# Largest eigenvalue by eleven matrix squarings in place of sixteen, with moved set-up loads and exchanged PSUM banks, in a two-layer graph kernel

## The reference, cut to what matters

```python
h = relu(layernorm(x));  x = x + layer0(h, adj, ...)      # x is (16, 512, 128), adj is (512, 512)
h = relu(layernorm(x));  x = x + layer1(h, adj, adj, ...)

def layer0(x, adj_mx, alpha_train, w, d, fc_in_w, fc_in_b):
    x0 = x
    h = einsum('bnd,ed->bne', x, fc_in_w) + fc_in_b
    alph = sigmoid(alpha_train)[:, None]
    w_eff = w * clip(d, 0, 1) @ w.T
    for _ in range(8):
        h = h + dt * (alph * 0.5 * (adj_mx @ h - h) + h @ w_eff - h + x0)
    return h

def layer1(x, L, adjacency, ...):
    lam_max = eigvalsh(L)[-1] + 1e-08                      # the largest eigenvalue of a 512x512 matrix
    L_norm = 2.0 * L / lam_max - eye(N)
    h = relu(layernorm((L_norm @ x) @ Wc + bc, g1, be1)); x1 = h + x
    q, k, v = (split_heads(x1 @ W) for W in (Wq, Wk, Wv))  # 4 heads of 32
    attn = softmax(where(adjacency > 0, q @ k.T / sqrt(32), -1e9))
    x2 = layernorm(x1 + (attn @ v) @ Wo + bo, g2, be2)
    return layernorm(x2 + gelu(x2 @ W1 + b1) @ W2 + b2, g3, be3)
```

## Time and profile before

| | |
|---|---|
| median of 3 runs | 951.16 us (950.97 to 957.17) |
| the profiled execution | 951.66 us, of which the span of the trace is 949.9 us |
| PE busy | 884.3 us (93%) |
| DVE busy | 650.7 us (69%) |
| ACT busy | 551.3 us (58%) |
| POOL busy | 325.0 us (34%) |
| mean granted PE clock | 0.984 of full speed |

### The profile page before, as it was taken

How to read it: one execution, slowest core, us unless ns; L and a number is a source line. 1 busy time by engine, 2 the same in 40 slices (tenths; PEclk the granted TensorE clock), 3 DMA queues, 4 the chain that set the end, 5 groups by cost and what they waited for, 6 DMA issues and landing times.

```text
span 949.9 us, 19236 instructions
## 1 busy us (share of the span) xinstructions
PE 884.3 (93%) x6854; PEld 723.6 (76%) x6854; DVE 650.7 (69%) x2075; ACT 551.3 (58%) x1210; POOL 325.0 (34%) x426
## 2 busy tenths in 40 slices
PE   5999999999999999987999999999999999888993
PEld 4878989898989888985677776767777777667782
DVE  5955453535354554635888888888989888886786
ACT  3223343434343332314888888888888887885574
POOL 3211111111111132301445445555555543313876
PEclk9999999999999989999999999999999999999998
DMA  3000000000000000230545555444445555500222
GB/s 97 1 12 12 12 12 13 11 12 12 12 12 12 12 23 1 70 65 18 128 124 133 135 134 135 118 110 110 107 106 122 134 134 134 135 2 2 56 57 67
DMA packets 47232, 61.73 MB, mean 65 GB/s; under 512 B 4377, under 2 KB 22050, under 8 KB 47138
## 3 DMA queue, kind: packets, MB, share of 16 engines
q1 hardware_dynamic: 46034, 60.38, 24.9%
q10 hardware_dynamic: 1104, 0.13, 0.1%
HBM read 39.53 MB, written 20.97 MB: 64 GB/s over the span
## 4 chain that ended last, share of the span: by engine, by line
PE 17%; DVE 11%; POOL 9%; issue 9%; ACT 7%; DVEq 0%; POOLq 0%; ACTq 0%
PE bank L1730 5%; DVE prob L1901 4%; PE bank L1750 3%; PE bank L1794 2%; ACT prob L1841 2%; POOL z_gain L317 2%; POOL z_norm L321 2%; POOL x_bo L1674 2%; PE bank L1717 2%; POOL rstd_b L202 1%; DVE z_std L298 1%; PE bank L353 1%; POOL rstd L202 1%; PE bank L349 1%; ACT probT L1830 1%
## 5 line engine op out<-in xcount | busy, mean ns | idle before, releaser
L1841 ACT ACTIVATE prob<-prob,low 128x512 f32<-128x512 f32 x256 | 184.0, 719 | 58.7 <-DVE low L1901 56.8
L1901 DVE CUSTOM_DVE_ANT_0 prob<-bank,mask 128x512 f32<-128x512 f32 x256 | 171.4, 684 | 27.6 <-PE bank L1717 26.2
L1730 PE MATMUL bank<-ident,prob 128*128 128x128 f32 x1024 | 162.1, 281 | 13.2 <-ACT probT L1830 12.9
L1730 PEld LDWEIGHTS bank<-ident,prob 128*128 128x128 f32 x1024 | 114.2, 141 | 59.0 <-issue 30.8
L1717 PE MATMUL bank<-k_stack,q_stack 128*128 128x512 f32 x256 | 122.6, 480 | 2.3 <-DVE low L1901 1.1
L809 PE MATMUL bank<-B_hi,halves 128*128 128x384 f32 x384 | 106.7, 339 | 0.7 <-DVE halves L1164 0.7
L1830 ACT ACTIVATE probT<-bank 128x512 f32<-128x512 f32 x176 | 102.4, 582 | 3.1 <-PE bank L1730 1.6
L780 PE MATMUL bank<-halves,P3T_hi 128*128 128x256 f32 x512 | 98.1, 293 | 3.4 <-DVE halves L1182 2.2
L963 ACT ACTIVATE Sq<-bank,trace_inv 128x512 fp32r<-128x512 f32 x64 | 43.9, 686 | 87.4 <-PE bank L764 87.4
L601 POOL TENSOR_SCALAR var_eps<-mv 128x4 f32<-128x4 f32 x16 | 3.6, 226 | 261.9 <-DVE mv L1115 261.9
L780 PEld LDWEIGHTS bank<-halves,P3T_hi 128*128 128x128 f32 x512 | 83.7, 198 | 6.3 <-DVE halves L1182 2.5
(11 more groups left out here) (251 smaller groups left out, 1964.3 us busy)
## 6 DMA issues: line engine op xcount, KB each, us to landing
k_stack<-bounce_q SPq DMA_DIRECT2D x64, 256.0 KB, 5.1
q_stack<-bounce_k SPq DMA_DIRECT2D x64, 256.0 KB, 7.5
bounce_q<-k_parts SPq DMA_DIRECT2D x16, 512.0 KB, 2.7
bounce_k<-q_parts SPq DMA_DIRECT2D x16, 512.0 KB, 3.3
x_in<-in_x_dram SPq DMA_DIRECT2D x16, 256.0 KB, 2.8
out_dram<-probT SPq DMA_DIRECT2D x16, 256.0 KB, 2.3
y<-in_adj_dram SPq DMA_DIRECT2D x4, 256.0 KB, 4.5
W1s<-in_L_gnn_W_dram SPq DMA_DIRECT2D x1, 128.0 KB, 2.6
```

Source lines behind the costliest of these rows:

```text
L1730: last = pe.transpose(psum[2 + u % 2][:, mt * P:(mt + 1) * P], prob[u % RING][:, mt * P:(mt + 1) * P], ident[:, :])
L1841: act.activation(prob[u % RING][:, :], prob[u % RING][:, :], ACT.Exp, bias=low[:, u % TURNED:u % TURNED + 1], scale=-1.0, accum_out=row_su ...
L1901: dve.tensor_tensor_reduce(prob[u % RING][:, :], psum[u % 2][:, :], mask[:, u // HEADS, :], 1.0, 3e38, ALU.add, ALU.min, low[:, u % TURNED ...
```

## The change

1. **Eleven squarings.** Six of them (q = 1 to 6) square S - c*I instead of S, where c is 0.45 times an estimate of the largest eigenvalue (the sum of the squared row sums over the sum of the row sums). ACT's copy of a row now also accumulates its row sums into `v` (`power_rows`). The trace of a shifted squaring brings three numbers over PE, and DVE makes seven more instructions on them, four of them on the diagonal blocks of the matrix; PE's first row of the squaring waits for all. Pairs 0 to 4 have 8 rows each and pair 5 has 4. The row sums at `LAM_PAIR` fall away.
2. **Set-up.** `alpha`, `d` and `fc_b` are loaded as six rows of 512 bytes and transposed by PE, one instruction more on PE and one copy on DVE. The spreading of the nine rows (PE and DVE) goes ahead of P3, into banks 4 to 6.
3. **Layer 1.** Spread uses bank 5 and q bank 4; the waits follow. The fourth tile of `normalise` goes from u = 15 to u = 0 of the next round; `split_b2` goes from round 16, u = 13 to round 15, u = 11.

```diff
 PAIRS = BATCH // 2
-ROWS_FIRST = ("T1a", "T2a", "C0a", "C1a", "T1b", "T2b", "C0b", "C2b")
-ROWS_3 = ("T1a", "Y1_0", "Y1_1", "T2a", "Y0_1", "C0a", "C1a", "C2a", "T1b", "T2b", "C0b", "C2b")
-ROWS_2 = ("T1a", "Y1_1", "T2a", "Y0_0", "C1a", "T1b", "T2b", "C1b")
-SQUARES = (ROWS_FIRST, ROWS_3, ROWS_3, ROWS_3, ROWS_3, ROWS_2)
-TRACES = (("T0a", "C3a"), *[("T0a", "Y0_0", "C3a")] * 4, ("T0a", "C0a"))
+ROW_PLACES = ("T1a", "T2a", "C0a", "C1a", "T1b", "T2b", "C0b", "C2b")
+SQUARES = (ROW_PLACES,) * 5 + (ROW_PLACES[:NT],)
+TRACES = (("T0a", "C3a"),) * 5 + (("T0a",),)
 LAST_SQUARED = len(SQUARES) - 1
 SQUARINGS = sum(len(rows) for rows in SQUARES) // NT
 LAM_PAIR, KEY_PAIR = LAST_SQUARED + 1, LAST_SQUARED + 2
-assert SQUARINGS == 2 * PAIRS and KEY_PAIR == PAIRS - 1
+SHIFT = 0.45
+SHIFTED = range(1, SQUARINGS - 4)
+assert KEY_PAIR == PAIRS - 1 and 2.0 ** (SQUARINGS - len(SHIFTED)) * (2 / (1 - SHIFT)) ** len(SHIFTED) >= 2.0 ** 16
...
                 pe.wait_ge(ident_ready, 1)
+                pe.wait_ge(small_loaded, 16 * 3)
+                pe.transpose(psum[6][:, 0:NT + 2], small_rows[:, :], ident[0:NT + 2, 0:NT + 2]).then_inc(setup_psum, 1)
                 pe.wait_ge(w_loaded, 16)
                 pe.transpose(psum[4][:, 0:D], w_in[:, :], ident[:, :]).then_inc(setup_psum, 1)
...
+                pe.wait_ge(B_step, STEPS + 1)
+                pe.wait_ge(one.rows_loaded, 16 * ROWS)
+                row_flat = one.row_in[:, :, :].rearrange("o r d -> o (r d)")
+                for c in range(3):
+                    if c == 2:
+                        pe.wait_ge(U_ready, GROUP)
+                    cols = min(N, ROWS * D - c * N)
+                    pe.matmul(psum[4 + c][:, 0:cols], ones[0:1, :], row_flat[:, c * N:c * N + cols], start=True,
+                              stop=True).then_inc(one.rows_spread, 1)
                 pe.wait_ge(PT_lo_ready, 2 * NT)
                 for mt in range(NT):
                     node_power(mt, P2T_parts, P3_psum)
...
+                pe.wait_ge(one.rows_copied, 3)
...
+                        cols = 3 if q in SHIFTED else 1
                         pe.wait_ge(trace_part_ready, q + 1)
-                        pe.matmul(SQ_BANK[:, 0:1], ones[:, :], trace_part[:, :], start=True,
+                        pe.matmul(SQ_BANK[:, 0:cols], ones[:, :], trace_part[:, 0:cols], start=True,
...
                     if step == (0, "T1a"):
-                        pe.wait_ge(v_ready, 1)
+                        pe.wait_ge(square_ready, NT * SQUARINGS)
...
                 act.dma_start(w_in[:, :], w).then_inc(w_loaded, 16)
-                act.dma_start(d_in[:, :], d.rearrange("(p o) -> p o", o=1)).then_inc(small_loaded, 16)
-                act.dma_start(alpha_in[:, :], alpha.rearrange("(t p) -> p t", p=P),
-                              allow_slow_non_contiguous=True).then_inc(small_loaded, 16)
-                act.dma_start(b_in[:, :], fc_b.rearrange("(p o) -> p o", o=1)).then_inc(small_loaded, 16)
+                act.dma_start(small_rows[0:NT, :], alpha.rearrange("(t p) -> t p", p=P)).then_inc(small_loaded, 16)
+                act.dma_start(small_rows[NT:NT + 1, :], d.rearrange("(o p) -> o p", o=1)).then_inc(small_loaded, 16)
...
                         if mt == 0:
-                            act.wait_ge(trace_step, 3 * q + 3)
-                        act.activation(Sq[1 - s][:, mt, :], SQ_BANK[:, :], ACT.Copy,
-                                       scale=trace_inv2[:, 0:1]).then_inc(square_ready, 1)
+                            act.wait_ge(trace_step, scales_until(q + 1))
+                        act.activation(Sq[1 - s][:, mt, :], SQ_BANK[:, :], ACT.Identity, scale=trace_inv2[:, 0:1],
+                                       accum_out=v[:, mt:mt + 1]).then_inc(square_ready, 1)
...
-                dve.wait_ge(small_loaded, 16 * 3)
-                dve.tensor_scalar(d_clip[:, :], d_in[:, :], 0.0, 1.0, ALU.max, ALU.min).then_inc(dve_setup, 1)
+                dve.wait_ge(setup_psum, turned_small)
+                dve.tensor_copy(small[:, :], psum[6][:, 0:NT + 2]).then_inc(dve_setup, 1)
                 dve.wait_ge(dve_setup, 1)
+                dve.tensor_scalar(d_clip[:, :], d_in, 0.0, 1.0, ALU.max, ALU.min).then_inc(dve_setup, 1)
...
+                dve.wait_ge(setup_psum, product_w)
+                dve.tensor_copy(W, psum[5][:, 0:D]).then_inc(power_ready, 1)
                 dve.wait_ge(alpha_exp, 1)
...
-                                         ALU.mult, ALU.add, trace_part[:, :]).then_inc(trace_part_ready, 1)
+                                         ALU.mult, ALU.add, trace_part[:, 0:1]).then_inc(trace_part_ready, 1)
+                dve.wait_ge(setup_psum, second_U)
+                dve.tensor_copy(U[:, :, 2], psum[6][:, 0:NT]).then_inc(U_ready, 1)
+                for c in range(3):
+                    cols = min(N, ROWS * D - c * N)
+                    dve.wait_ge(one.rows_spread, c + 1)
+                    dve.tensor_copy(one.bc_all[:, :, :].rearrange("p r d -> p (r d)")[:, c * N:c * N + cols],
+                                    psum[4 + c][:, 0:cols]).then_inc(one.rows_copied, 1)
                 for i in range(STEPS):
                     for j in range(STEPS - i):
...
-                    if q is not None:
-                        dve.wait_ge(trace_psum, q + 1)
-                        dve.tensor_scalar(trace[:, :], SQ_BANK[:, 0:1], TINY, None, ALU.max).then_inc(trace_step, 1)
-                        dve.wait_ge(trace_step, 3 * q + 1)
+                    if q is None:
+                        return
+                    done = scales_until(q)
+                    dve.wait_ge(trace_psum, q + 1)
+                    dve.tensor_scalar(trace[:, :], SQ_BANK[:, 0:1], TINY, None, ALU.max).then_inc(trace_step, 1)
+                    dve.wait_ge(trace_step, done + 1)
+                    at_least(dve, square_ready, NT * q)
+                    if q in SHIFTED:
+                        dve.scalar_tensor_tensor(out=mean_power[:, :], in0=trace[:, :], scalar=1.0 / N,
+                                                 in1=SQ_BANK[:, 1:2], op0=ALU.mult, op1=ALU.max
+                                                 ).then_inc(trace_step, 1)
                         dve.reciprocal(trace_inv[:, :], trace[:, :]).then_inc(trace_step, 1)
-                        dve.wait_ge(trace_step, 3 * q + 2)
-                        at_least(dve, square_ready, NT * q)
+                        dve.wait_ge(trace_step, done + 2)
+                        dve.reciprocal(mean_inv[:, :], mean_power[:, :]).then_inc(trace_step, 1)
+                        dve.wait_ge(trace_step, done + 3)
+                        dve.tensor_tensor(out=trace_inv2[:, :], in0=trace_inv[:, :], in1=trace_inv[:, :],
+                                          op=ALU.mult).then_inc(trace_step, 1)
+                        dve.wait_ge(trace_step, done + 4)
+                        dve.tensor_scalar(neg_shift[:, :], SQ_BANK[:, 2:3], mean_inv[:, 0:1], -SHIFT, ALU.mult,
+                                          ALU.mult).then_inc(trace_step, 1)
+                        dve.wait_ge(trace_step, done + 6)
+                        for t in range(NT):
+                            own = Sq[q % 2][:, t, t * P:(t + 1) * P]
+                            dve.scalar_tensor_tensor(out=own, in0=ident[:, :], scalar=neg_shift[:, 0:1],
+                                                     in1=own.bitcast(F32), op0=ALU.mult, op1=ALU.add
+                                                     ).then_inc(trace_step, 1)
+                    else:
+                        dve.reciprocal(trace_inv[:, :], trace[:, :]).then_inc(trace_step, 1)
+                        dve.wait_ge(trace_step, done + 2)
                         dve.tensor_tensor(out=trace_inv2[:, :], in0=trace_inv[:, :], in1=trace_inv[:, :],
                                           op=ALU.mult).then_inc(trace_step, 1)
...
                         dve.wait_ge(square_ready, NT * (q + 1))
+                        if q + 1 in SHIFTED:
+                            dve.tensor_reduce(trace_part[:, 1:2], v[:, :], AX.X, ALU.add)
+                            dve.tensor_tensor_reduce(scratch4[:, :], v[:, :], v[:, :], 1.0, 0.0, ALU.mult, ALU.add,
+                                                     trace_part[:, 2:3])
                         dve.tensor_tensor_reduce(diagonal[:, :, :], diagonal_of(Sq[1 - s]).bitcast(F32), ident_tiles,
-                                                 1.0, 0.0, ALU.mult, ALU.add, trace_part[:, :]
+                                                 1.0, 0.0, ALU.mult, ALU.add, trace_part[:, 0:1]
...
-AT_Y_MOMENTS, AT_H = 9, (11, 12, 13, 15)
+AT_Y_MOMENTS, AT_H = 9, (11, 12, 13)
...
-AT_W1_LO, AT_SPLIT_B2 = (BATCH, 5), (BATCH, 13)
+AT_W1_LO, AT_SPLIT_B2 = (BATCH, 5), (BATCH - 1, 11)
...
                             pe.wait_ge(rinv_ready, e + 1)
-                            pe.wait_ge(x1T_ready, min(r + 1, BATCH) if isinstance(r, int) else r + 1)
```

(13 more changed lines are left out.)

69 lines of the change are left out of this document (28 added, 41 removed).

## The result

The changed kernel takes 922.61 us (median of 4 runs, 921.45 to 925.83) against 953.27 for the kernel before on the same chip, a ratio of 0.968 (95% interval 0.966 to 0.971), about 30 us less. The profiled execution is the longest of the four, 925.83 us with a span of 924.0; the other three have spans of 919.6 to 921.0.

The account below looks back on a forecast made before the run. PE was taken to bound the kernel, busy without a break in layer 0. The terms summed to -33.0 us, giving 918.7 against the profiled 951.66, or 918.2 by the runs' median, stated as 918; range 910 to 930.

Parts of the forecast that it names:

- Five squarings fewer: Layer 0, PE: each squaring with its trace is worth 4.19 us, so five give -21.0 us.
- rival (2): Squarings covered more than they cost: PE meets waits the rows hid, half of 21 us returns; about 931 us, chance 0.09.
- DVE's chain at shifted squarings: Layer 0: PE waits for DVE's chain of about 2.2 us, mostly covered by `first_power`; +0.6 us; `C2_lo` ready near 330.5, needed near 330.8.
- Row sums at pair 6: Pair 6: DVE's 2.28 us reduction goes, so PE's product with S starts earlier; -1.8 us.
- The clock at pair 6: Pair 6: without the 1.8 us idle, the low-clock stretch has half its length; -1.6 us, bounds 0 and -3.3.
- Spreading moved: Set-up: PE's 1.41 us wait for `P3T_lo` ahead of the spreading goes; -1.4 us, bounds 0 and -3.1.
- Small loads: Set-up: row loads land earlier, so PE's first adjacency transposes start near 8.2 instead of 10.06; -1.8 us.
- Layer 1: Layer 1 rounds: most of the spread's wait for `x1T`, 6.4 us over 14 rounds, is gained; -4.5 us.
- rival (1): Small terms are given back: layer 1 waits for `probT` instead, the clock stays low as long; 927 us, chance 0.17.
- split_b2: Round 16: PE's 1.71 us idleness behind this DVE work goes; -1.5 us, bounds 0 and -3.3.
- Rival (3): Layer 0: stops ahead of shifted rows bring the 0.50 clock level for pairs 0 to 3; over 951 us, chance 0.02.
- my last sentence: Prediction is wrong if PE waits over 0.5 us at shifted squarings, `q_lo` waits appear, or low-clock windows between 60 and 300 us.

Follow-up runs that it names:

- No shift: The changed kernel with the six shifts left out, so eleven plain squarings; median 922.08 us.
- Spread dealt: The changed kernel with one spreading product behind each of P3's first three tiles, DVE's copies likewise; ratio 0.972 to the kernel before.
- three: The changed kernel with pair 5's rows in its b half, the quotient's instructions ahead of DVE's first Y1 sum, spreading dealt through P3; median 920.38 us.
- S dealt: The changed kernel with pair 6's S products dealt out between `first_power`'s products and the quotient's instructions ahead of DVE's first Y1 sum; median 929.20 us.
- U mixed: The changed kernel with the one-column products with U and the spreading products dealt out between P3's products; median 924.03 us.

## Why the prediction was right, and which steps were off

The time came 4.6 us above the forecast of 918 and inside the range; against before, about 30 us less where 33 were forecast. Of the 7.1 us that the profiled execution falls short (25.9 against 33.0), 1.7 lie in set-up and pair 0, 1.8 in pair 5 and 3.7 in pair 6.

- **Five squarings fewer: right, 19.1 instead of 20.4 us.** Pairs 1 to 4 gave 4.16 us each. The step that was off is "one squaring with its trace is worth 4.19 us" for pair 5: there it gave 2.44, for the four rows left in the a half uncovered two waits in the b half. This is rival (2) in small, in the one pair with an empty half; with the rows moved it gives 3.80.
- **DVE's chain at shifted squarings: right mechanism, cost 0 instead of 0.6.** I worked it out as 2.2 us; it took 1.9, and left 0.65 us. The `C2_lo` margin held. No shift confirms it by 0.03 us over four pairs.
- **Row sums at pair 6: right, about 1.4 instead of 1.8 us.** The product with S starts 0.22 us behind the last `first_power` matmul. With half of the low stretches taken off, pair 6 took 51.8 us before (55.20 with 6.8 at 0.50) and takes 50.4 now (55.54 with 10.2). The time was not all kept: the quotient behind it is set by DVE's order and POOL's statistics, which I had not followed. "Ask what is late next" was left out at this step.
- **The clock at pair 6: half a hit.** In five of the runs the low stretch is 3.4 us, as I took it, and pair 6 takes 52.0 to 52.2 us, 3.1 less than before (forecast 3.4). In the profiled execution it is 6.8 + 3.4 us, pair 6 is as long as before, and that alone is 3.4 of this profile's shortfall. The bounds were wide enough, the assumption that one execution stands for all was not.
- **Spreading moved: the wait right, the clock wrong.** "What goes is PE's wait of 1.41 us" came true, and at equal clock the move is worth 1.5 us (seven kernels against three). But the product itself doubled its time, 4.20 for 2.20, and P3 behind it ran its first 5 us at half speed. I had named the lengthened weak stretch and then priced it at nothing; the 3.4 us more at 0.50 cost 1.7. From P2 to pair 1 it took 68.9 us against 68.6, so nothing is left of the 1.4 in this profile. Four of the other kernels in this order had 6.8 us more than before. Spread dealt has 68.2 (89.17 - 21.02), by its clock and not by its order.
- **Small loads: the number right, by two misses that cancel.** P2 starts at 20.89 instead of 22.70 us, 1.81 less, as forecast; 19.7 to 21.3 in the other runs with the new loads, 23.70 in the one with the old, which has 3.4 us at 0.50 ahead of P2. But the transposes of the adjacency matrix start at 7.10, not near 8.2, and below the 7.7 that I took for a floor: its loads landed 3.4 us after their issue by the median, where they took 4.5 before. Of these 2.96 us, 1.15 are lost again by P2 (13.79 us from there instead of 12.64, both with 2.0 us idle); the sum had no term for that, and its cause stays open. The row loads were all there at 5.05 us, not at the 6.0 to 6.5 that I took. From the fixed cost of about 2.0 us in the Trainium skill, "DMA: Bandwidth & Descriptors", section "Anatomy of one DMA — SWDGE (gpsimd) path", I had estimated 4.1. The -2.4 of that estimate is not what this profile shows, but P2's start scatters by 1.6 us over the twelve kernels with the new loads, more than the difference.
- **Layer 1: right, 3.75 instead of 4.2 us for 13 rounds.** 0.29 us a round instead of 0.32. The `probT` wait did not take it back, which answers rival (1), and no wait for `q_lo` appeared.
- **split_b2: right, about 2.0 instead of 1.5 us** in round 16. The other 1.0 of the 3.0 us by which round 16 fell goes with the low stretch of the earlier trace rows, which round 16 no longer has; round 15 gives back 1.1 us, and whether this edit has a part in that is open.
- **Rival (3), a low level over the squarings: not seen.** The trace has 1.00 from 60 to 300 us although PE's rows wait in one bank. The short idle times that the Trainium skill describes ("TensorE: Matmul & The Clock Gate", section "A second HAM failure mode: psum-queue depth-cycling") hardly occurred here, 0.35 us in 240, so its rule was not put to the test. In nine of the other twelve kernels a stretch of 3.4 us starts between 63.2 and 66.2 us, in pair 0, as one did in the kernel before at 55.2; by the letter of my last sentence this would have counted against the forecast, and it costs 1.5 us (pair 0 37.6 instead of 36.1).

## What to carry to other kernels

A piece of work taken off the busiest engine is worth its own time only where the rest of that stretch never waits; look at the place it leaves, half pair by half pair, and put what remains where the waits are. Follow a released wait to the next consumer's whole chain, on other engines too (here DVE's order and POOL's statistics), before it is counted. When an engine's clock changes within a run, first take half of its low stretches off the stages where it is never idle, and only then compare: here this turned ranges that lay over each other (68.6 to 72.0 and 68.7 to 70.4) into two groups, each at most 0.3 us wide, and 1.5 us apart. Totals that differ by seven microseconds for one and the same program don't show edits of one or two.

## What the runs showed of the hardware

- One program on the same chip (spread dealt): 920.37 us at a mean granted clock of 0.988, and three times 927.3 to 927.5 at 0.978. How much of an execution runs at the 1.2 GHz level was not fixed by the program.
- The level fell after stretches of one-column products (before, changed, spread dealt), after idle times of 1.6 to 4.7 us (three, S dealt), and in U mixed with 1.83 us idle ahead. In nine kernels it fell in pair 0, 0.4 to 1.4 us behind 2.84 us of products with three contracted rows (L754) and with PE busy; in the changed kernel and U mixed it did not fall behind the same products. One-column products dealt out between 512-column ones were not followed by it (S dealt). In three, 3.63 us of one-column products from 308.94 on were followed by full clock up to 317.4. What exactly brings it was not found; ahead of the kernels' ends the stretches lasted 3.4 us, or two or three times that.
- ACT's copy with `accum_out` costs a second instruction of its own, in the timeline of the changed kernel:

```profile
132.16 0.69 ACT L973 ACTIVATE Sq<-bank,trace_inv 128x512 fp32r<-128x512 f32 x1 [2.95 <-PE bank L775]
...
132.75 0.19 ACT L973 ACTIVATION_READ_ACCUMULATOR Sq<-bank,trace_inv 128x1 f32 x1
```
